# Pair building by single tiles, with a bucket's products kept in PSUM and its room read from a table

## The chip, the cores and the metric

The kernel runs on one core of a Trainium2 chip. The metric is the device time of one launch in microseconds (us). The engines are named as in the profile: PE (TensorE, with PEld for its weight loads), DVE (VectorE), ACT (ScalarE), POOL (GpSimd) and SP (the DMA queue). Each has a sequencer that takes its instructions in order; register instructions, loads of registers and waits are done there, and the profile marks them with a q (PEq, PEldq, DVEq).

## The reference, cut to what matters

Four graph layers work on 625 nodes of 512 features and 20000 edges. Every layer sums over edges into the node an edge ends in. The first two layers (a mean over neighbours, and two relational convolutions) need the edges only through sums over node pairs:

```python
# layer 0: mean over neighbours
neighbor_sum = segment_sum(x[src], dst)
h = concatenate([x, neighbor_sum / max(count, 1)]) @ W.T + b
# layer 1, twice: relational convolution, 8 relations, 4 bases
hb = einsum('nd,bdo->bno', h, basis)
m = sum_b comp[etype, b] * hb[b][src] * norm
out = segment_sum(m, dst) + bias + h @ loop_w
```

So the kernel builds nine matrices over (src, dst) once: for each of 2 x 4 coefficients the sum of `comp[etype, b] * edge_weight` over the edges of a node pair, and the count of edges. Layers 0 and 1 are then dense products with them. Layers 2 and 3 go over the edges by gathers and are not touched by the change.

## The kernel before

The program is a list of stages (`STAGES`, L2695): `constants`, `place_edges`, `order_pairs`, `build_pairs`, `layers_0_and_1`, `layers_2_and_3`. Between two stages all engines meet at a barrier (L2708). Inside a stage each engine has its own list of instructions, written out by hand, and semaphores order them.

The nodes an edge can end in are cut into 40 buckets of 16 (`CELL`): 5 blocks of 8. `place_edges` counts the edges of each bucket, gives each edge a slot of the sorted order, and a place (lane, tile) among tiles of 128 edges for the pair building. A bucket takes whole items of two tiles (`PAIR` = 256 edges), so `NI` = 118 items and `PT` = 236 tiles. It also writes `column_of_item`, which bucket an item belongs to, into one row of int32.

`order_pairs` brings keys, weights and coefficients of the edges into tile order with one-hot matmuls (20 batches, DVE writes the one-hots at L591 to L603, PE multiplies, ACT writes a third kind at L539) and computes from them, 236 columns wide, the nine values of each edge (`pair_high`, bf16, and `pair_rest`, fp16, what bf16 leaves). Beside it ACT and POOL clear `pairs` (L485, L532), and POOL sends the first `FIRST` = 54 columns of edge records to DRAM (`scatter_records`, L686).

`build_pairs` (L706) is the stage of the change. `pg.pairs` is 128 sources x 5 source blocks x 9 matrices x 640 ends, f32 in SBUF. For item g:

- DVE (L799) and, for the second tile in three items of four, ACT (L776, L780) write `src_hot`, the one-hot of each edge's source, 128 x 640.
- POOL (L765) writes `cell_high` and `cell_rest`: the one-hot of the end within its bucket times the nine (eight) values.
- PE (L741, L744) multiplies, for each of two tiles and five source blocks, `src_hot` by both: 20 matmuls of 144 or 128 columns, into one of two PSUM buffers `pairs_ps`.
- DVE loads the item's column from `column_of_item` into a register (L804) and adds the 720 columns of PSUM to `pairs` at that column (L809).

Semaphores: `used` (PE is done with an item), `cells_made`, `first_hot`, `second_hot`, and `added` (the PSUM buffer is free again). The loops are hardware loops (`Fori`), four items in a round.

Later, in layer 3, PE loads registers in the same form: `value_load` at L1919, twice in a row, and then computes a matmul operand's address from each (L1936).

Of the kernel before, what the change touches and what calls it, by code (L numbers as in the profile page):

```python
# [12 lines left out]
FP32 = mybir.dt.float32  # L13
BF16 = mybir.dt.bfloat16
# [28 lines left out]
PAIR = 2 * P  # L43
NI = (EDGES + NB * (PAIR - 1)) // PAIR + NB * (P // CELL - 1)
NI += (2 - NI) % 4
PT = 2 * NI
EARLY = EC // 2
LANDED = EC // 2
FIRST = 54
# [24 lines left out]
def constants(pg):  # L74
# [3 lines left out]
    pg.iota_src = pg.sb("iota_src", [P, PW], FP16)  # L78
    pg.iota_lane = pg.sb("iota_lane", [P, PT], BF16)
# [38 lines left out]
    pg.column_of_item = pg.sb("column_of_item", [1, NI], I32, pg.pair_once)  # L118
# [17 lines left out]
    with nc.semaphore("filled") as filled, nc.Block() as block:  # L136

        @block.gpsimd
        def _(pool):
            nc.gpsimd.iota(pg.iota_free[:, :], [[1, P]], base=0, channel_multiplier=0,  # L140
                           allow_small_or_imprecise_dtypes=True)
            nc.gpsimd.iota(pg.iota_lane[:, :], [[1, PT]], base=0, channel_multiplier=0,
                           allow_small_or_imprecise_dtypes=True)
            nc.gpsimd.iota(pg.iota_src[:, :], [[BN, NB], [1, P]], base=0, channel_multiplier=0,
# [21 lines left out]
def place_edges(pg):  # L166

    nc = pg.nc
    with ExitStack() as ctx:
# [32 lines left out]
        reached = pg.sb("reached", [P, BUCKETS], ctx=ctx)  # L202
        bucket_of = pg.sb("bucket_of_item", [P, 1], ctx=ctx)
        row_ps = ctx.enter_context(nc.psum_tensor("row_ps", [P, 512], FP32))
        table_ps = ctx.enter_context(nc.psum_tensor("table_ps", [P, 512], FP32))
# [28 lines left out]
        def _(pool):  # L234
            nc.gpsimd.iota(bucket_no[:, :], [[1, BUCKETS]], base=0, channel_multiplier=0,
                           allow_small_or_imprecise_dtypes=True)
            nc.gpsimd.iota(pg.iota_twice[:, :, :], [[1, PT], [0, 2]], base=0, channel_multiplier=0,
                           allow_small_or_imprecise_dtypes=True)
# [21 lines left out]
        def _(act):  # L260
# [23 lines left out]
            for ends, at in ((pg.edge_record[0:EP, 0:EARLY, SRC:SRC + 2], slice(0, EARLY)),  # L284
                             (pg.late_ends, slice(EARLY, EARLY + FIRST)), (pg.last_ends, slice(EARLY + FIRST, EC))):
                nc.scalar.copy(ends[:, :, 0], ints[:, 0, at])
                nc.scalar.activation(ends[:, :, 1], ints[:, 1, at], ACT.Identity, bias=pg.ones[0:EP, 0:1])

        @block.tensor
        def _(pe):  # L290
# [5 lines left out]
            nc.tensor.matmul(table_ps[0:1, 0:P], bucket_of[:, :], pg.ident[:, :], start=True,  # L296
                             stop=True).then_inc(sem["tables_turned"], 1)

        @block.vector
        def _(dve):  # L300
# [10 lines left out]
            for b in range(2, NB):  # L311
# [56 lines left out]
            link(nc.vector.tensor_scalar(bounds_i[:, 1, :], bounds[:, 1, :], float(PAIR - 1), None, ALU.add))  # L368
            link(nc.vector.tensor_scalar(bounds_i[:, :, :], bounds_i[:, :, :], 8, None, ALU.arith_shift_right))
            link(nc.vector.tensor_copy(bounds[:, :, :], bounds_i[:, :, :]))  # L370
            link(nc.vector.tensor_tensor(items[:, :], bounds[:, 1, :], bounds[:, 0, :], ALU.subtract))
            link(nc.vector.scalar_tensor_tensor(out=items[:, :], in0=total[:, :], scalar=0.0, in1=items[:, :],
                                                op0=ALU.is_gt, op1=ALU.mult))
            link(nc.vector.tensor_tensor_scan(out=item_last[:, :], data0=items[:, :], data1=zero[:, :],
                                              initial=0.0, op0=ALU.add, op1=ALU.add))
            nc.vector.tensor_scalar(reached[:, :], item_last[:, :], pg.lane_no[:, 0:1], None, ALU.is_le)
            link(nc.vector.tensor_tensor(offset[:, :], bounds[:, 0, :], item_last[:, :], ALU.subtract))
            nc.vector.tensor_reduce(bucket_of[:, :], reached[:, :], AX.X, ALU.add).then_inc(sem["tables_made"], 1)
            link(nc.vector.tensor_tensor(offset[:, :], offset[:, :], items[:, :], ALU.add))
            link(nc.vector.scalar_tensor_tensor(out=shift[0:EP, :], in0=offset[0:EP, :], scalar=float(P),  # L380
                                                in1=unit_size[0:EP, :], op0=ALU.add, op1=ALU.mult))
            link(nc.vector.tensor_tensor(shift[0:EP, :], shift[0:EP, :], start[0:EP, :], ALU.add))
            link(nc.vector.tensor_tensor(shift[0:EP, :], shift[0:EP, :], row_ps[0:EP, 0:BUCKETS], ALU.add))
            for b in range(BUCKETS):
# [19 lines left out]
            nc.vector.scalar_tensor_tensor(out=pg.pair_tile[:, :], in0=unit[:, :], scalar=-2.0,  # L404
                                           in1=slot_i[:, :], op0=ALU.mult, op1=ALU.add)

            dve.wait_ge(sem["tables_turned"], 1)
# [2324 lines left out]
```

## Time and profile before

| | us |
|---|---|
| median of 3 runs | 2236.05 |
| lowest, highest | 2234.85, 2241.26 |
| the profiled execution | 2239.19 |
| its span, first to last instruction | 2237.5 |
| `build_pairs` in it, barrier to barrier (188.0 to 383.3) | 195.3 |
| `order_pairs` in it, barrier to barrier (65.4 to 188.0) | 122.6 |

Busy time is given by engine; a PE matmul's listed duration runs from its start to its modelled end, and several are under way at once, so the spacing of starts tells what one costs. The times of the stages are read from the barrier's instructions. A stage ends when its last engine arrives.

### The profile page before, as it was taken

How to read it: one execution, taken by the hardware profiler on the slowest of the kernel's cores; microseconds unless marked ns; L12 is line 12 of the kernel's file. 1: busy time of each engine (PE TensorE's matmuls, PEld its weight loads, DVE VectorE, ACT ScalarE, POOL GpSimd, SP SyncE). 2: the span in 40 equal slices, each digit the busy share in tenths (PEclk: the TensorE clock that was granted, in tenths of full speed). 3: DMA queues.
4: the chain of work that ended last, by engine and by line, in shares of the span. 5: the costliest groups of instructions: out<-in, count | busy, mean ns of one | idle time of the engine just before them, and what ended most of it. 6: DMA issues, size and time to landing. Idle time of an engine off the chain costs nothing. (4 is left out here: it accounts for less than half of the span.)

```text
span 2237.5 us, 35489 instructions
## 1 busy us (share of the span) xinstructions
PE 1957.2 (87%) x11394; PEld 1133.0 (51%) x11507; DVE 1573.5 (70%) x2245; ACT 1274.9 (57%) x2059; POOL 1473.2 (66%) x1123
## 2 busy tenths in 40 slices
PE   0796887989898769999999978999999999999875
PEld 0775776456565524444444444555555555555432
DVE  8998998633333557777777743888888888888723
ACT  1667777021122246666666633777877777777622
POOL 1787777777600057777777713799889898998530
PEclk9999999989999879999999989999999999999988
DMA  2411001132234234333333204332222222222000
GB/s 117 161 22 46 0 0 43 35 106 60 64 106 113 61 108 140 109 95 93 90 94 90 80 11 128 97 95 76 72 83 72 78 74 71 83 73 77 5 0 23
DMA packets 78495, 165.22 MB, mean 74 GB/s; under 512 B 15999, under 2 KB 41016, under 8 KB 77220
## 3 DMA queue, kind: packets, MB, share of 16 engines
q0 software_dynamic: 34560, 94.69, 15.7%
q1 hardware_dynamic: 43800, 68.78, 9.4%
q8 instruction: 79, 1.29, 0.2%
q14 instruction: 56, 0.46, 0.1%
HBM read 139.86 MB, written 23.39 MB: 73 GB/s over the span
## 5 line engine op out<-in xcount | busy, mean ns | idle before, releaser
L939 PE MATMUL e_two_ps<-w,e_first 128*128 128x512 bf16 x1261 | 382.8, 380 | 4.7 <-issue 0.4
L686 POOL DMA_INDIRECT sorted_records<-edge_record,slot_row x160 | 248.4, 1552 | 69.1 <-issue 54.9
L2371 POOL DMA_INDIRECT e_got<-src_table,e_idx x168 | 225.8, 1344 | 67.2 <-issue 34.1
L939 PE MATMUL e_two_ps<-w,e_first_low 128*128 128x512 bf16 x672 | 255.2, 380 | 0.0
L1707 ACT ACTIVATE u_msg<-u_t,slot_record 128x128 f32<-128x128 f32 x672 | 214.4, 395 | 71.4 <-DVE u_t L1772 71.4
L1888 POOL TENSOR_TENSOR e_first_low<-e_first 128x1024 bf16<-128x1024 f32 x84 | 232.2, 2765 | 19.3 <-DVE e_first L2072 14.9
L1620 POOL TENSOR_TENSOR total<-total,u_part 125x1024 f32 x84 | 198.0, 2357 | 66.9 <-ACT u_part L1715 57.5
L1893 POOL TENSOR_TENSOR e_msg_low<-e_act 128x1024 bf16<-128x1024 f32 x84 | 189.3, 2253 | 39.1 <-DVE e_act L2084 37.7
L1610 POOL DMA_INDIRECT u_got<-up_table,u_idx x168 | 162.0, 964 | 60.0 <-POOL u_idx L1604 32.5
L939 PEld LDWEIGHTS e_two_ps<-w,e_first 128*128 128x128 bf16 x1344 | 128.3, 98 | 141.9 <-issue 2.2
L2079 DVE TENSOR_TENSOR e_lin<-e_two_ps,bias 128x512 f32<-128x512 f32 x168 | 115.3, 687 | 118.4 <-PE e_two_ps L939 118.4
L1671 PE MATMUL u_sum_ps<-u_msg,u_hot 128*125 128x512 f32 x336 | 179.9, 617 | 14.4 <-ACT u_msg L1707 14.4
L741 PE MATMUL pairs_ps<-cell_high,src_hot 128*128 128x144 bf16 x1180 | 152.8, 227 | 41.8 <-DVE src_hot L799 21.9
L1673 PE MATMUL u_sum_ps<-u_msg,u_hot 128*125 128x512 f32 x336 | 172.5, 595 | 0.0
L1997 ACT ACTIVATE e_act<-e_act,log_bias 128x1024 f32<-128x1024 f32 x84 | 96.5, 1148 | 104.7 <-DVE e_act L2061 104.7
L744 PE MATMUL pairs_ps<-cell_rest,src_hot 128*128 128x128 f16 x1180 | 152.2, 220 | 0.0
L741 PEld LDWEIGHTS pairs_ps<-cell_high,src_hot 128*128 128x128 bf16 x1180 | 115.4, 98 | 58.0 <-POOL cell_rest L765 55.7
L1366 PE MATMUL rc_out<-pairs 125*125 125x512 bf16 x600 | 135.6, 379 | 1.2 <-PE rc_mix L939 0.2
L1772 DVE TENSOR_TENSOR u_t<-u_tp_ps,u_got 128x256 f32<-128x256 f32 x168 | 70.6, 420 | 90.9 <-PE u_tp_ps L1660 88.9
L1444 DVE TENSOR_TENSOR pairs<-rc_mix,pairs 125x512 bf16<-125x512 f32 x40 | 27.7, 691 | 149.1 <-ACT pairs L1412 149.1
L1993 ACT ACTIVATE e_act<-e_lin 128x1024 f32<-128x1024 f32 x84 | 88.9, 1058 | 68.1 <-DVE e_lin L2079 68.1
L809 DVE TENSOR_TENSOR pairs<-pairs,pairs_ps 128x720 f32 x118 | 106.4, 902 | 21.5 <-PE pairs_ps L744 14.2
(373 smaller groups left out, 4725.6 us busy)
## 6 DMA issues: line engine op xcount, KB each, us to landing
conv_w<-in_L_gnn_basis_dram SPq DMA_DIRECT2D x8, 1024.0 KB
sorted_records<-pairs SPq DMA_DIRECT2D x5, 1344.0 KB, 10.4
later_w<-in_L_gnn_W_dram SPq DMA_DIRECT2D x6, 1024.0 KB
attr_parts<-h SPq DMA_DIRECT2D x21, 256.0 KB, 2.1
e_attrT<-attr_parts SPq DMA_DIRECT2D x42, 128.0 KB
e_dst_all<-dst_row SPq DMA_DIRECT2D x42, 125.0 KB
edge_record<-in_edge_floats_dram SPq DMA_DIRECT2D x1, 3125.0 KB
pairs<-in_edge_floats_dram SPq DMA_DIRECT2D x1, 3125.0 KB
```

What stands on the lines that cost most here:

```text
L686: pg.nc.gpsimd.indirect_dma_start(out=pg.sorted, out_offset=bass.IndirectOffsetOnAxis(ap=pg.slot_row[:, j:j + 1], axis=0), in_=pg.edge_rec ...
L741: nc.tensor.matmul(ps[h][:, sb, 0:(COEFS + 1) * CELL], hot, high[:, h, k, :, :].rearrange("p n d -> p (n d)"), start=(k == 0 and sb % 2 == ...
L744: last = nc.tensor.matmul(ps[h][:, sb, 0:COEFS * CELL], hot, rest[:, h, k, :, :].rearrange("p n d -> p (n d)"), start=False, stop=(k == 1 ...
L939: last = nc.tensor.matmul(out, lhsT, rhs, start=(n == 0), stop=(n == len(pairs) - 1))
L1610: nc.gpsimd.indirect_dma_start(out=got[:, b, :], out_offset=None, in_=tableU, in_offset=bass.IndirectOffsetOnAxis(ap=idx[:, r, k:k + 1], a ...
L1620: nc.gpsimd.tensor_tensor(into, into, part[:, n % 2, :], ALU.add).then_inc(added, 1)
L1671: nc.tensor.matmul(sum_ps[k // TH][0:BN, 0:D], hot[:, g % HOTS * TG + k, :], msg[:, k, 0:D], start=(k % TH == 0), stop=(k % TH == TH - 1))
L1673: nc.tensor.matmul(sum_ps[k // TH][0:BN, D:M], hot[:, g % HOTS * TG + k, :], msg[:, k, D:M], start=(k % TH == 0), stop=(k % TH == TH - 1)) ...
L1707: last = nc.scalar.activation(msg[:, k, at * MUL:(at + 1) * MUL], t12[:, k % 2, of], ACT.Copy, scale=pg.record[:, bass.ds(t, 1), Y + m])
L1888: nc.gpsimd.tensor_tensor(first_low[:, r % 2, 2 * u:2 * u + 2, :], full, upper(full), ALU.subtract).then_inc(low1, 1)
L1893: nc.gpsimd.tensor_tensor(msg_low[:, u, :, :], act2[:, u, :, :], upper(act2[:, u, :, :]), ALU.subtract).then_inc(low2, 1)
L2371: pg.nc.gpsimd.indirect_dma_start(out=self.got[:, r * TG + k, :], out_offset=None, in_=table, in_offset=bass.IndirectOffsetOnAxis(ap=self. ...
```

## The change

- Items of two tiles go. A bucket takes whole tiles of 128 edges and at least one: `PT` = 196 tiles.
- A bucket's products stay in PSUM over all its tiles. `pairs_ps` is one tensor of three rooms, each two banks (three source blocks in one, two in the other). Two rooms are used in turn by the buckets; room 0 takes what is not wanted.
- Which bucket a tile belongs to is known only from the data, so `place_edges` writes `tile_table`, four int32 for each tile: how many buckets must have been copied out, the tile's room, the room to open and the room to close (0 where the bucket goes on). PE loads the four into registers for each tile. A matmul of two columns (`mark`) opens or closes each bank, so a tile has 10 products and 4 marks.
- ACT copies a bucket out once, two copies for 40 buckets each, after loading from `tiles_through` the tile that ends it. DVE's additions and loads go, so `pairs` need not be cleared: POOL's and ACT's clearing in `order_pairs` goes.
- DVE writes `src_hot` for every tile; ACT writes none. Six buffers of it, three pairs of cell buffers.
- 42 columns of records are sent in `order_pairs` and 12 in `build_pairs`, one after every third pair of tiles.
- All loops of the stage are written out.

```diff
-PAIR = 2 * P
-NI = (EDGES + NB * (PAIR - 1)) // PAIR + NB * (P // CELL - 1)
-NI += (2 - NI) % 4
-PT = 2 * NI
+PT = (EDGES + NB * (P - 1)) // P + NB * (P // CELL - 1)
+PT += PT % 2
-FIRST = 54
+FIRST, IN_ORDER = 54, 42
...
-    pg.column_of_item = pg.sb("column_of_item", [1, NI], I32, pg.pair_once)
+    pg.tile_table = pg.sb("tile_table", [1, 4, PT], I32, pg.pair_once)
+    pg.tiles_through = pg.sb("tiles_through", [1, BUCKETS], I32, pg.pair_once)
...
+            nc.vector.tensor_scalar(pg.tiles_through[:, :], item_last[0:1, :], 1.0, None, ALU.add)
...
+            link(nc.vector.tensor_scalar(by_tile[:, 1, :], before_i[:, :], 1.0, None, ALU.add))
+            nc.vector.tensor_tensor(by_tile[:, 2:4, :], changed[:, :, :], by_tile[:, 1:2, :].broadcast_to([P, 2, 2]),
+                                    ALU.mult).then_inc(sem["tables_made"], 1)
...
             nc.gpsimd.memset(zero[:, :], 0.0).then_inc(zeroed, 1)
-            nc.gpsimd.memset(pairs[:, 0:CLEARED], 0.0)
             pool.wait_ge(pg.emptied, 16 * 5)
-            scatter_records(pg, range(0, FIRST))
+            scatter_records(pg, range(0, IN_ORDER))
...
-                if i >= WAITED:
-                    act.wait_ge(pg.emptied, 16 * 5)
-                    at = CLEARED + (i - WAITED) * size
-                    clear(pairs[:, at:at + size])
...
+            def mark(room, bank, begins):
+                at = slice(room, room + 1) if isinstance(room, int) else bass.ds(room, 1)
+                return nc.tensor.matmul(ps[:, at, bank, BANK * WIDE:BANK * WIDE + 2].rearrange("p r c -> p (r c)"),
+                                        pg.ident16[:, :], pg.ident16[:, 0:2], start=begins, stop=not begins)
+
+            def of_tile(k, t, top):
+                return nc.tensor.value_load(pg.tile_table[0:1, k, t:t + 1], min_val=1 if k == 0 else 0, max_val=top)
...
+            for t in range(PT):
+                before = of_tile(0, t, BUCKETS)
+                room = of_tile(1, t, 2)
+                opened = of_tile(2, t, 2) if t >= 1 else room_of(0)
+                closed = of_tile(3, t, 2) if t + 1 < PT else room_of(BUCKETS - 1)
+                pe.wait_ge(cells_made, t // 2 + 1)
+                pe.wait_ge(hots_made, t + 1)
+                pe.wait_ge(freed, before)
+                for bank in range(2):
+                    mark(opened, bank, True)
+                    for sb in range(bank * BANK, min(NB, (bank + 1) * BANK)):
+                        hot = src_hot[:, t % DEEP, sb * P:(sb + 1) * P]
+                        for cells in (high, rest):
+                            begin = sb % BANK * WIDE
+                            into = ps[:, bass.ds(room, 1), bank, begin:begin + cells.shape[3] * CELL]
+                            nc.tensor.matmul(into.rearrange("p r c -> p (r c)"), hot,
+                                             cells[:, t // 2 % TWO, t % 2, :, :].rearrange("p n d -> p (n d)"),
+                                             start=False, stop=False)
+                    last = mark(closed, bank, False)
                 last.then_inc(used, 1)
...
+            for b in range(BUCKETS):
+                if b + 1 < BUCKETS:
+                    through = nc.scalar.value_load(pg.tiles_through[0:1, b:b + 1], min_val=1, max_val=PT + 1)
+                    act.wait_ge(used, through)
...
+                    last = nc.scalar.copy(pg.pairs[:, sbs, :, b * CELL:(b + 1) * CELL],
+                                          full.rearrange("p (s n d) -> p s n d", n=COEFS + 1, d=CELL))
+                last.then_inc(freed, 1)
...
+            for t in range(PT):
+                if t >= DEEP:
+                    dve.wait_ge(used, t - DEEP + 2)
+                nc.vector.tensor_scalar(src_hot[:, t % DEEP, :], names, pg.pair_src[:, t:t + 1], None,
+                                        ALU.is_equal).then_inc(hots_made, 1)
```

On PE, where an item begins inside `build_pairs`, this stands before (L738 and L749 are register instructions for the semaphore's value, ISA is such an instruction):

```order
L741 MATMUL pairs_ps<-cell_high,src_hot 128x144 [waits pairs_first_hot,pairs_added,pairs_cells_made]
L744 MATMUL pairs_ps<-cell_rest,src_hot 128x128
L741 MATMUL pairs_ps<-cell_high,src_hot 128x144
L744 MATMUL pairs_ps<-cell_rest,src_hot 128x128
L741 MATMUL pairs_ps<-cell_high,src_hot 128x144
L744 MATMUL pairs_ps<-cell_rest,src_hot 128x128
```

And this stands on PE after the change where a tile begins (the second tile; `tile_table` is the table, L733 the marks, L757 the products):

```order
L737 TENSOR_LOAD tile_table
L737 ISA x2
L737 TENSOR_LOAD tile_table
L737 ISA x2
L737 TENSOR_LOAD tile_table
L737 ISA x2
L737 TENSOR_LOAD tile_table
L737 ISA x2
L733 ISA [waits pairs_freed,pairs_hots_made,pairs_cells_made]
L733 MATMUL pairs_ps<-ident 128x2
L757 ISA
L757 MATMUL pairs_ps<-cell_high,src_hot 128x144
```

Four loads, each with two register instructions behind it, now stand in front of every tile's first matmul; the rest of the tile is nine single ISA instructions (the two last rows' kind) with 14 matmuls among them.

On DVE the same stage before, one item of the loop:

```order
L799 ISA [waits pairs_used]
L799 TENSOR_SCALAR src_hot<-pair_names_ps,pair_src 128x640
L804 ISA
L804 TENSOR_LOAD column_of_item
L804 ISA x2
L806 REGISTER_ALU
L809 ISA [waits pairs_added,pairs_used]
L809 TENSOR_TENSOR pairs<-pairs,pairs_ps 128x45x16
```

and on ACT after, the first two buckets:

```order
L785 ACTIVATE h<-x,x_nmr,x_rs 125x512 x5
L789 TENSOR_LOAD tiles_through
L789 ISA x2
L796 COPY pairs<-pairs_ps 128x27x16 [waits pairs_used]
L796 COPY pairs<-pairs_ps 128x18x16
L789 TENSOR_LOAD tiles_through
```

The load with its two register instructions has left DVE, where it stood once for two tiles; ACT has one for each bucket, and PE four for each tile.

## Rows read from the trace of the kernel before

**Rows 1.** Windows (order_pairs, build_pairs): stretch, busy us of engines, clock, DMA:

```profile
core 0: us, PE busy (x) PEld busy (x) DVE busy (x) ACT busy (x) POOL busy (x), PEclk, DMA share, GB/s
65.00:187.00 122.00, 105.38 (x843) 85.29 (x843) 115.62 (x202) 82.12 (x215) 99.50 (x56) 0.97 0.21 65
188.00:383.30 195.30, 157.67 (x2360) 142.00 (x2360) 171.84 (x265) 151.11 (x185) 146.47 (x236) 0.99 0.03 11
```

**Rows 2.** Waits in 188 to 383: who for whom, us, times, longest:

```profile
PEld pairs_ps L741 <- POOL cell_rest L765: 55.7, 88, 9.5
POOL cell_high L765 <- PE pairs_ps L744: 42.7, 87, 1.6
PE pairs_ps L741 <- DVE src_hot L799: 21.9, 57, 0.6
```

**Rows 3.** Tile pairs_ps: operation, count, ns min/median/max, first and last start us:

```profile
L741 PE MATMUL pairs_ps<-cell_high,src_hot x1180: 222/226/328, 189.8 to 380.2; 128*128 128x144 bf16 x197
L809 DVE TENSOR_TENSOR pairs<-pairs,pairs_ps x118: 894/904/906, 192.4 to 380.6; 128x720 f32 x118
```

**Rows 4.** Timeline of PE, first and last of an item's 20 matmuls:

```profile
282.53 0.22 PE L741 MATMUL pairs_ps<-cell_high,src_hot 128*128 128x144 bf16 x1 [0.38 <-POOL cell_rest L765]
...
283.65 0.22 PE L744 MATMUL pairs_ps<-cell_rest,src_hot 128*128 128x128 f16 x1
```

**Rows 5.** Lines L765 (POOL) and L799 (DVE), columns as in Rows 3:

```profile
L765 POOL TENSOR_TENSOR cell_high<-pair_cell,pair_high x118: 666/669/673, 188.5 to 377.8; 128x288 bf16 x118
L765 POOL TENSOR_TENSOR cell_rest<-pair_cell,pair_rest x118: 611/614/617, 189.1 to 378.4; 128x256 f16 x118
L799 DVE TENSOR_SCALAR src_hot<-pair_names_ps,pair_src x147: 541/545/550, 188.2 to 378.5; 128x640 bf16<-128x640 bf16 x147
```

**Rows 6.** Line L1919, PE's register loads in layer 3, all of them:

```profile
L1919 PEldq TENSOR_LOAD <-block_of_half x168: 295/298/486, 1372.1 to 2089.3; - x168
L1919 PEldq FUSED_REGOPS  x168: 151/151/165, 1372.6 to 2089.6; - x168
L1919 PEldq SEQ_ASSERT  x168: 18/18/32, 1372.9 to 2089.8; - x168
```

**Rows 7.** Line L1919 in 1599 to 1601, one pair of loads in a row:

```profile
L1919 PEldq TENSOR_LOAD <-block_of_half x2: 298/298/298, 1599.4 to 1600.0; - x2
L1919 PEldq SEQ_ASSERT  x2: 18/18/18, 1600.0 to 1600.6; - x2
```

**Rows 8.** Line L1936 in 1600.5 to 1601.5, the address instructions behind that pair:

```profile
L1936 PEldq FUSED_REGOPS  x4: 51/58/65, 1600.7 to 1601.1; - x4
```

**Rows 9.** Tile count_ps, 50 matmuls of one column in a row:

```profile
L939 PE MATMUL count_ps<-ones,pairs x50: 165/165/187, 388.2 to 389.6; 125*128 125x1 bf16 x50
```

**Rows 10.** Line L804, DVE's register loads in build_pairs:

```profile
L804 DVEq TENSOR_LOAD <-column_of_item x118: 298/305/566, 188.7 to 378.9; - x118
```

**Rows 11.** Lines by form, an ACT copy out of PSUM, busy us and mean ns:

```profile
L565 ACT CAST pair_high<-pair_coef_ps 128x472 bf16<-128x472 f32 x2 | 1.9, 1058 | 0.0
```

**Rows 12.** Timeline, the first of the 54 records' scatters, the last, DVE's last:

```profile
77.38 1.37 POOL L686 DMA_INDIRECT sorted_records<-edge_record,slot_row  x1 [0.73 <-DMA sorted_records<-pairs]
...
183.13 1.18 POOL L686 DMA_INDIRECT sorted_records<-edge_record,slot_row  x1 [0.30 <-issue]
...
184.15 0.66 DVE L679 TENSOR_TENSOR pair_rest<-hT,pair_high 128x472 f16<-128x472 f32 x1 [0.21 <-ACT pair_high L567]
```

**Rows 13.** Lines L593 and L664 (DVE in order_pairs), columns as in Rows 3:

```profile
L593 DVE TENSOR_TENSOR pairs<-hT,pair_tile x20: 1133/1134/1137, 66.2 to 147.2; 125x1888 bf16<-125x1888 bf16 x20
L664 DVE SCALAR_TENSOR_TENSOR hT<-h,pair_comp,hT x28: 452/462/515, 169.2 to 181.0; 128x236 f32<-128x236 f32 x28
```

**Rows 14.** Timeline, an iota that goes, and a small DVE operation of place_edges:

```profile
1.41 0.68 POOL L144 IOTA iota_src<- 128x640 f16 x1
...
60.88 0.24 DVE L399 TENSOR_SCALAR key_part_i<-h 125x160 int32<-125x160 int32 x1
```

## What the change should do to the time

> **What bounds the kernel now.** I read the windows view first, by stage. `build_pairs` lasts 195.3 us, and in it no engine is full: DVE 172, PE 158, ACT 151, POOL 146 us [rows 1]. The waits view says why: the engines wait on each other in a ring, PE's weight loads for POOL's `cell_rest` 55.7 us, POOL for PE 42.7 us, PE for DVE's `src_hot` 21.9 us [rows 2]. Each has two buffers. The first and last of DVE's 118 additions give 188.2 / 117 = 1.61 us for an item [rows 3]. PE's own need is smaller: a listed matmul lasts 226 ns, but 20 of them start within 282.53 to 283.65, so one costs 1.12 / 19 = 0.059 us [rows 4] and an item 1.18 us. The end of the chain of waits lies in layer 3, behind barriers; each stage is a piece of the sum of its own, so I work by stages and read in each which engine comes last.
>
> **What the matmuls, one-hots and copies cost after the change.** There are 196 tiles instead of 236. PE's array has ten products at 0.059 us and four marks. A mark is nearest to the 50 one-column matmuls that start within 388.2 to 389.6, 0.029 us each, weights loaded anew each time [rows 9]. That is 0.59 + 0.12 = 0.71 us a tile, 139 us in all. POOL has 98 pairs of tiles at 0.669 + 0.614 us = 126 us [rows 5], and twelve scatters of about 1.2 us [rows 12], together 140 us. DVE has 196 operations at 0.545 us = 107 us at most [rows 5], and its additions (118 x 0.904 = 107 us) are gone [rows 3]. ACT has 80 copies. No row shows one of 432 or 288 f32 columns into strided places; by the copy of 472 columns at 1.06 us [rows 11] a bucket costs at most 2.1 us, 85 us in all, and it lies beside 4.9 tiles of PE's work thanks to the two rooms. Only the last bucket's copies are on the path. So far the stage would end at POOL's and PE's 140 us.
>
> **What PE's sequencer costs after the change.** This is the term I put the forecast on. In front of every tile stand four `value_load`s on PE. `build_pairs` of before has none on PE, but layer 3 has 168 of just this form there, always two in a row. One load is a TENSOR_LOAD of 298 ns, a register instruction of 151 ns and an assertion of 18 ns, 0.467 us [rows 6]. With the gaps between them it is more: the two loads start at 1599.4 and 1600.0, the second assertion at 1600.6, and the first address instruction behind at 1600.7 [rows 7, 8]. Two loads thus took 1.3 us, 0.65 us each. They run one behind the other and overlap with nothing on the sequencer. In layer 3 they are hidden because the array has many 512-column matmuls queued; here the whole array work of a tile is 0.71 us. Four loads are 2.60 us a tile.
>
> Then come nine address instructions, each in front of one or two matmuls that are handed over. Four of these start within 1600.7 to 1601.1, three spacings in 0.4 us, one weight load and matmul in each [rows 8]: 0.14 us. Nine are 1.26 us. Five more matmuls at 0.03 us [rows 9] are 0.15 us, and the separate wait instruction about 0.05 us. The sequencer needs 2.60 + 1.26 + 0.15 + 0.05 = 4.06 us for a tile, against 0.71 us of the array. A queue cannot help, since every tile has the same surplus. 196 x 4.06 = 796 us. To that I add 3.5 us for the first loads' fill, the last bucket's copies and the barrier: 799 us for the stage, 604 us more than 195.3. DVE, POOL and ACT wait for PE and cost nothing; should the clock granted to a PE that idles this much be 1.2 GHz instead of 2.4, the array's 0.71 us doubles to 1.4 and still hides.
>
> The price of a load has ends. From below, if the gaps vanished: 4 x 0.467 us, and nine address instructions at their own 0.058 us [rows 6, 8], with 14 matmuls at 0.03: 1.87 + 0.52 + 0.42 = 2.81 us a tile. From above, the slowest load in any row, DVE's 566 ns [rows 10], every time: 4 x (0.65 - 0.298 + 0.566) + 1.46 = 5.13 us. Nothing below zero is open: the instructions are added and DVE's removed loads lay beside other work. I take 0.65 because rows 7 and 8 are the same engine and the same three instructions. Read with the rounding of those rows (0.1 us on 1.3 and on 0.4), a load is 0.60 to 0.70 and an address instruction 0.10 to 0.17, which makes 3.5 to 4.5 us a tile.
>
> The Trainium skill, "DMA: Bandwidth & Descriptors", section on latency and other measured facts, gives `tensor_load` a floor of about 600 ns, to be amortized by unrolling. The trace does not agree with that as the duration of the instruction (298 ns), though it nearly does for the whole sequence of 0.65 us. By the page's figure as a duration, an estimate from it: 4 x (0.65 - 0.298 + 0.600) + 1.46 = 5.27 us a tile, 237 us above my sum.
>
> **The stages ahead.** In `order_pairs` two engines end close together: POOL's 54 scatters run from 77.38 to 183.13, 2.0 us each, and DVE's last operation ends at 184.8 [rows 12], while the barrier opens at 188.0 [rows 1]. A barrier alone takes at most 1.8 us (383.3 less the last addition's end at 381.5 [rows 1, 3]), so it was POOL's last records that it waited for. With 42 scatters POOL is done by about 160, so DVE sets the end. DVE loses by width: 1568 elements instead of 1888 in 20 operations of 1.134 us, at most 0.19 each or 3.8 us [rows 13]; and of the 28 operations of 0.462 us and some thirty others, all 236 wide and now 196, I count 0.05 each, 3.5 us with `pair_cell`. So DVE ends at about 177.5, the barrier opens by 179.3 at the latest, and that is 9 us earlier. The clearing goes from POOL and ACT, but POOL waited for the emptied DRAM anyway (the first scatter's releaser is a DMA [rows 12]), and ACT waited for DVE; nothing for that. `constants` loses two iotas, 1 us by the row of 0.68 [rows 14]; `place_edges` gains some eight small DVE operations at up to 0.24 [rows 14], hidden to about half by SP's issues: 1 us. PE's transposes of the table lie beside DVE. Sum ahead: -9 to -10 us. Layers 0 to 3 have the same instructions, behind a barrier as before; nothing for them.
>
> **Sum.** 2237.5 + 604 - 10 = 2831.5 us of span. The profiled run took 2239.2, which is 3.1 above the median of 2236.05, so against the median: 2236 + 594 = **2830 us**.
>
> **The rivals.** *The loads hide (ends on the other side).* Place: PE's sequencer between two tiles. If it could hand over a tile's loads while the array works, such that what is not hidden is under (195.3 - 3.5) / 196 = 0.98 us a tile, the stage would not get longer. Fully hidden, the stage ends by POOL's and PE's 140 us and 7 for fill and gaps, 147: 2236 - 48 - 10 = 2178 us. For it speaks that in rows 6 layer 3 loses nothing to its loads, and that the code keeps a tile's work together. Against it: there they have 20 matmuls of over 0.2 us to hide behind, here 14 of 0.05. Chance 0.06.
>
> *Cheap sequencer (still slower).* The gaps vanish where the array is idle, 2.81 us a tile: 551 + 3.5 us, 2236 + 359 - 10 = 2585 us. Against it: in rows 7 and 8 the sequencer was not held up by the array either, for the loads need no place in its queue. Chance 0.04.
>
> *Dear loads.* The slow loads of rows 10 are the rule: 5.13 us a tile, 1009 us, 2236 + 814 - 10 = 3040 us. The median of 298 over 168 loads speaks against it. Chance 0.03. By the floor in the Trainium skill, "DMA: Bandwidth & Descriptors", section on latency and other measured facts, an estimate of this kind comes to 3067 us.
>
> *The change does not do what it says.* The instruction order shows the four loads, the 14 matmuls and the 80 copies, so this I leave at nothing.
>
> **How the numbers follow.** The forecast, sequencer bound at about 4 us a tile, has 0.87. Its own range by 3.5 to 4.5 us a tile is 2830 - 110 to 2830 + 90, rounded out to 2715 to 2930; I give that 0.93 within the case, so the range holds 0.81 and need not reach to the rivals. The measurement can tell about 0.3% of the time (7 us) from no change. Slower by more: 0.87 + 0.04 + 0.03 = 0.94, less 0.01 for a mixed case that ends on par. Same: 0.01. Faster: 0.06.
>
> **What would show it.** Right: `build_pairs` near 800 us; L737 with 782 TENSOR_LOADs on PE's sequencer near 0.3 us, starting 0.65 us apart; PE busy a fifth of the stage or less between bursts, with POOL and DVE waiting for PE at L776 and L808, and ACT's buckets some 20 us apart. `order_pairs` shorter by about 9 us with DVE last. Wrong: matmuls of successive tiles without gaps, waits of PE for POOL as the longest, or loads that start closer than 0.5 us. If the array's work showed as the longer one, with the clock at its lower level and matmuls over 0.2 us apart, the place would be right and the mechanism wrong. If a later stage changed by over 5 us, the sum by stages would be wrong.

## The result and the profile after

The changed kernel takes 2798.4 us (median of 4 runs, 2793.45 to 2799.39) against 2237.1 us before (4 runs, 2234.85 to 2241.26). The ratio is 1.250, with a 95% interval of 1.248 to 1.253. The prediction was 2830 us with a range of 2715 to 2930.

The windows view of after, by stage (constants and `place_edges` together, `order_pairs`, `build_pairs`, the layers); its columns are those of [rows 1]:

```profile
core 0: us, PE busy (x) PEld busy (x) DVE busy (x) ACT busy (x) POOL busy (x), PEclk, DMA share, GB/s
0.00:62.70 62.70, 4.64 (x20) 2.77 (x20) 53.74 (x111) 13.53 (x19) 8.13 (x28) 0.88 0.34 143
62.70:174.40 111.70, 92.04 (x843) 77.23 (x843) 106.84 (x201) 65.72 (x198) 66.40 (x43) 0.93 0.21 70
174.40:942.30 767.90, 294.90 (x2749) 257.59 (x2750) 107.48 (x197) 36.75 (x87) 136.22 (x209) 0.50 0.01 4
942.30:2797.70 1855.40, 1702.36 (x8298) 905.03 (x8298) 1233.10 (x1673) 1029.07 (x1641) 1217.56 (x802) 0.96 0.28 79
```

and the same view of before for the layers, which [rows 1] leaves out:

```profile
383.30:2237.50 1854.20, 1692.54 (x8185) 904.74 (x8298) 1232.84 (x1673) 1028.86 (x1641) 1218.61 (x802) 0.96 0.28 79
```

The layers are the same within 1.2 us. The whole difference lies in one stage: `build_pairs` lasts 767.9 us where it lasted 195.3 [rows 1]. In it POOL is busy for 136 us, DVE for 107, ACT for 37, all less than before, and PE's 295 us of busy time cover 38% of it. No engine in the view is full. An engine's busy time leaves out what its sequencer does, and PE's sequencer is what is full here. The lines of PE's sequencer, by line (L737 the loads, L749 the wait, L733 the addresses of the marks, L757 those of the products), with count, ns min/median/max, first and last start in us:

```profile
L737 PEldq TENSOR_LOAD <-tile_table x782: 293/300/491, 174.6 to 937.6; - x196
L737 PEldq FUSED_REGOPS  x782: 146/151/165, 175.1 to 937.9; - x196
L737 PEldq SEQ_ASSERT  x782: 18/18/28, 175.3 to 938.2; - x196
L749 PEldq EVENT_SEMAPHORE  x196: 51/51/51, 176.7 to 938.3; - x196
L733 PEldq FUSED_REGOPS  x780: 46/53/65, 177.3 to 938.9; - x195
L757 PEldq FUSED_REGOPS  x980: 46/46/51, 176.8 to 939.1; - x196
```

The wait stands once in each tile: 938.3 less 176.7 over 195 is 3.906 us for a tile, where the forecast had 4.06. The same lines in one tile near the middle, in three windows: its loads, its wait and its nine addresses, and the loads of the next tile:

```profile
L737 PEldq TENSOR_LOAD <-tile_table x4: 296/297/301, 498.5 to 500.5; - x4
...
L749 PEldq EVENT_SEMAPHORE  x1: 51/51/51, 501.1 to 501.1; - x1
...
L757 PEldq FUSED_REGOPS  x5: 46/46/51, 501.4 to 502.1; - x5
...
L733 PEldq FUSED_REGOPS  x4: 46/53/65, 501.2 to 502.3; - x4
...
L737 PEldq TENSOR_LOAD <-tile_table x3: 303/303/305, 502.4 to 503.7; - x3
```

From the first load (498.5) to the wait (501.1) it is 2.6 us for four loads, 0.65 us each. The wait takes 0.1 us, and from the first address (501.2) to the next tile's first load (502.4) it is 1.2 us for nine addresses, 0.13 us each. All 14 matmuls of the tile are handed over in that time. The waits view of after, from 180 us on, says who stands still for it:

```profile
ACT pairs L796 <- PE pairs_ps L733: 729.5, 40, 22.7
DVE src_hot L808 <- PE pairs_ps L733: 634.8, 189, 3.5
POOL cell_high L776 <- PE pairs_ps L733: 605.5, 95, 6.7
PEld pairs_ps L733 <- issue: 499.3, 195, 2.7
PE pairs_ps L733 <- issue: 433.5, 180, 2.6
```

Three engines wait for PE, and PE waits for "issue", which means for nothing that the profile shows. The ring of [rows 2], in which each waited for the other, is gone. (The view puts 34.9 us in 15 tiles down to POOL: it names the one that came last of those that a tile asks for, and the sum of 2.6, 0.1 and 1.2 us leaves no room for a wait.) ACT has 40 waits of at most 22.7 us, one for each bucket. The timeline shows the burst of the tile above:

```profile
501.34 0.18 PE L733 MATMUL pairs_ps<-ident 128*128 128x2 bf16 x1 [2.46 <-issue]
501.47 0.30 PE L757 MATMUL pairs_ps<-cell_high,src_hot 128*128 128x144 bf16 x1
501.56 0.31 PE L757 MATMUL pairs_ps<-cell_rest,src_hot 128*128 128x128 f16 x1
...
502.63 0.21 PE L733 MATMUL pairs_ps<-ident 128*128 128x2 bf16 x1
```

2.46 us of nothing, then 14 matmuls within 1.29 us. Their starts are 0.10 us apart in the mean (those of two products in a row 0.08 to 0.12), where they were 0.059 us apart before [rows 4]. The granted clock in this stage is 0.50 (the windows view above), the lower of the two levels, 1.2 GHz. PE idled 2.5 us of every 3.9.

In `order_pairs`, 111.7 us in the windows view, the records end early and DVE ends last (timelines of POOL and DVE; [rows 12] before):

```profile
155.20 1.19 POOL L684 DMA_INDIRECT sorted_records<-edge_record,slot_row  x1 [0.30 <-issue]
...
172.50 0.57 DVE L677 TENSOR_TENSOR pair_rest<-hT,pair_high 128x392 f16<-128x392 f32 x1 [0.16 <-ACT pair_high L566]
```

Where a stage is timed from barrier to barrier by the barrier's own instruction on POOL, as in what follows, the numbers are: `order_pairs` 122.6 before and 110.6 after, `build_pairs` 195.3 and 767.8.

### The profile page after: what moved, and what is told of

It is laid out like the page before. It is cut to its first block and busy times, and to the rows that moved or that the text cites. A ratio compares the mean times of both kernels' runs of the same rounds, so it can differ in the third digit from the quotient of the medians.

```text
span 2797.7 us, 38255 instructions
## 1 busy us (share of the span) xinstructions
PE 2093.9 (75%) x11909; PEld 1242.6 (44%) x11909; DVE 1501.2 (54%) x2181; ACT 1145.1 (41%) x1945; POOL 1428.3 (51%) x1081
## 5 line engine op out<-in xcount | busy, mean ns | idle before, releaser
L733 PE MATMUL pairs_ps<-ident 128*128 128x2 bf16 x788 | 124.2, 193 | 475.3 <-issue 433.5
L808 DVE TENSOR_SCALAR src_hot<-pair_names_ps,pair_src 128x640 bf16<-128x640 bf16 x196 | 107.5, 550 | 637.3 <-PE pairs_ps L733 635.8
L928 PE MATMUL e_two_ps<-w,e_first 128*128 128x512 bf16 x1344 | 403.7, 382 | 0.0
L776 POOL TENSOR_TENSOR cell_high<-pair_cell,pair_high 128x288 bf16<-128x288 bf16 x98 | 65.5, 668 | 623.7 <-PE pairs_ps L733 605.5
L796 ACT COPY pairs<-pairs_ps 128x432 f32<-128x432 f32 x80 | 32.8, 462 | 729.5 <-PE pairs_ps L733 729.5
L733 PEld LDWEIGHTS pairs_ps<-ident 128*128 128x128 bf16 x788 | 100.7, 139 | 506.9 <-issue 506.9
L757 PE MATMUL pairs_ps<-cell_rest,src_hot 128*128 128x128 f16 x980 | 250.1, 314 | 0.0
L757 PE MATMUL pairs_ps<-cell_high,src_hot 128*128 128x144 bf16 x980 | 246.9, 312 | 0.1
L2360 POOL DMA_INDIRECT e_got<-src_table,e_idx x168 | 211.9, 1261 | 67.2 <-issue 33.9
L1882 POOL TENSOR_TENSOR e_msg_low<-e_act 128x1024 bf16<-128x1024 f32 x84 | 198.1, 2358 | 47.5 <-DVE e_act L2073 46.5
```

Of the source, the lines that this page charges most:

```text
L733: return nc.tensor.matmul(ps[:, at, bank, BANK * WIDE:BANK * WIDE + 2].rearrange("p r c -> p (r c)"), pg.ident16[:, :], pg.ident16[:, 0:2] ...
L757: nc.tensor.matmul(into.rearrange("p r c -> p (r c)"), hot, cells[:, t // 2 % TWO, t % 2, :, :].rearrange("p n d -> p (n d)"), start=False ...
L928: last = nc.tensor.matmul(out, lhsT, rhs, start=(n == 0), stop=(n == len(pairs) - 1))
L1882: nc.gpsimd.tensor_tensor(msg_low[:, u, :, :], act2[:, u, :, :], upper(act2[:, u, :, :]), ALU.subtract).then_inc(low2, 1)
L2360: pg.nc.gpsimd.indirect_dma_start(out=self.got[:, r * TG + k, :], out_offset=None, in_=table, in_offset=bass.IndirectOffsetOnAxis(ap=self. ...
```

## The experiments

**Theory:** the time of the stage is the time of PE's sequencer for a tile, the sum of its loads, its wait and its address instructions; nothing of it lies beside the array, and no other engine counts. **Rivals:** the lower clock or the structure with marks and long accumulation costs the time; the loads only wait for data; another engine's work is slow. The first five experiments take parts of that sum away one at a time, or put them into the kernel before. These five and the one after them were executed once each, so what they show rests on differences of many microseconds and on the stage times in their own traces.

### Two loads in place of four

```diff
-                opened = of_tile(2, t, 2) if t >= 1 else room_of(0)
-                closed = of_tile(3, t, 2) if t + 1 < PT else room_of(BUCKETS - 1)
+                opened = closed = room
```

> The changed kernel (2798 us) with two of PE's four register loads in front of each tile, and the room to open and to close taken from the tile's own room; it leaves out what a bucket's earlier tiles added, the rest of the work is the same. Seven address instructions in a tile instead of nine. Theory (PE's sequencer takes the loads one after the other, 0.65 us each, and 0.13 us for an address instruction, and the array's work hides behind): 2 x 0.65 + 2 x 0.13 = 1.57 us less in each of 196 tiles, 308 us less, 2490 us. Rival (the marks and the array at its lower clock set the pace): 14 matmuls as before, so 2798 us. Rival (what costs is a fixed latency for a group of loads, not each load): under 100 us less.

Measured: 2489.4 us, `build_pairs` 462.5 us. The loads (392 in place of 782) and the addresses of the marks, of which a tile now needs two in place of four:

```profile
L737 PEldq TENSOR_LOAD <-tile_table x392: 295/302/493, 175.2 to 632.8; - x196
...
L733 PEldq FUSED_REGOPS  x392: 46/56/65, 176.9 to 634.2; - x196
```

Two loads at 0.65 us and two addresses at 0.13 us are 1.56 us less, and 3.91 less 1.56 is 2.35 us a tile. The wait's instruction goes from 176.8 to 633.4, so the tile took 2.34 us. The array has the same 14 matmuls, and the clock is still 0.50:

```profile
180.00:630.00 450.00, 288.53 (x2695) 252.49 (x2693) 104.08 (x189) 32.30 (x80) 131.51 (x202) 0.50 0.02 7
```

So neither is the bound. The waits view of this kernel names DVE for PE's idle time (149.6 us in 179 waits). This is a way of counting: the wait asks for three things and the view names the one that came last of them. DVE itself waited 338.7 us for PE, and the loads, the wait and the addresses fill the 2.34 us by themselves.

### Three of the four loads without the check of their bounds

```diff
-                return nc.tensor.value_load(pg.tile_table[0:1, k, t:t + 1], min_val=1 if k == 0 else 0, max_val=top)
+                if k == 0:
+                    return nc.tensor.value_load(pg.tile_table[0:1, k, t:t + 1], min_val=1, max_val=top)
+                return nc.values_load(pg.tile_table[0:1, k, t:t + 1], engines=[mybir.EngineType.PE],
+                                      min_val=0, max_val=top,
+                                      skip_runtime_bounds_check_because="place_edges clamps every entry of the table")
```

> The changed kernel with all four loads, but three of them without the bound check (the register instruction of 151 ns and the assertion of 18 ns behind the load). Theory of single instructions in order: each unchecked load takes 0.36 us from its start to the next instead of 0.65, 3 x 0.29 = 0.87 us less in a tile, 170 us less, 2628 us. Rival (the load's answer is what is waited for, and loads in a row overlap when nothing reads their register): three loads in a row cost little more than one, up to 0.3 us less each, down to 2500 us. Rival (array or marks set the pace): 2798 us.

Measured: 2638.3 us, `build_pairs` 600.0 us. The stage is 167.8 us shorter, near the expected 170; the total is 10 us above the expectation mostly because the layers of this run were 7 us longer. The three loads of one tile, lines of PE's sequencer in 500 to 503.5:

```profile
L739 PEldq TENSOR_LOAD <-tile_table x3: 296/302/302, 501.5 to 502.2; - x3
```

Without the register instruction and the assertion behind it a load takes 0.36 us to the next one: 0.30 of its own and 0.06 of gap. So 0.29 of the 0.65 us were the check of the bounds, and the loads run one behind the other even where nothing stands between them: they start 0.36 us apart and last 0.30.

### One load that fills four registers

```diff
-    pg.tile_table = pg.sb("tile_table", [1, 4, PT], I32, pg.pair_once)
+    pg.tile_table = pg.sb("tile_table", [1, PT, 4], I32, pg.pair_once)
...
+                _, (before, room, opened, closed) = nc.values_load_multi_w_load_instructions(
+                    pg.tile_table[0:1, t, :], engines=[mybir.EngineType.PE], min_val=0, max_val=BUCKETS,
+                    skip_runtime_bounds_check_because="place_edges clamps every entry of the table")
+                before = nc.s_assert_within(before, 1, BUCKETS)
...
```

> The changed kernel with the table turned, so that one load fills all four registers of a tile, and only the value that PE waits against is checked (0 loads fewer in what they deliver, same results). Three unchecked loads cost 160 us less than checked ones. Theory (it is the number of load instructions that costs, 0.36 us each with its gap): one load and its check 0.65 us, nine address instructions 1.2 us, a wait 0.1 us, 1.96 us a tile against 3.91, 382 us less than 2798, so 2416 us. Rival (the price is for each register filled, so four in one cost four times the 0.3 us): 0.9 us more a tile, 2590 us. Still above the kernel before either way, since nine address instructions alone are 1.2 us a tile.

Measured: 2402.1 us, `build_pairs` 375.0 us. Of all tiles:

```profile
L743 PEldq TENSOR_LOAD <-tile_table x196: 327/331/525, 173.9 to 544.3; - x196
```

One load of four registers lasts 331 ns, 30 ns more than a load of one. 370.4 us over 195 is 1.90 us a tile: 0.39 us from the load to the next instruction, 0.17 for the assertion that is left, 0.11 for the wait and 1.20 for the nine addresses make 1.87. This halves the stage (375.0 of 767.8), takes back 396 of the 561 us that the change lost in all, and is still 163 us slower than before: nine addresses alone are 1.20 us a tile, 235 us in all, more than the whole stage of before.

### The rooms fixed when the kernel is built

```diff
+        def bucket_of(t):
+
+            return t * BUCKETS // PT
...
-                before = of_tile(0, t, BUCKETS)
-                room = of_tile(1, t, 2)
-                opened = of_tile(2, t, 2) if t >= 1 else room_of(0)
-                closed = of_tile(3, t, 2) if t + 1 < PT else room_of(BUCKETS - 1)
+                before = bucket_of(t) + 1
+                room = room_of(bucket_of(t))
+                opened = room if t == 0 or bucket_of(t - 1) != bucket_of(t) else 0
+                closed = room if t + 1 == PT or bucket_of(t + 1) != bucket_of(t) else 0
...
```

(the address of each product's room and what ACT waits for become constants in the same way)

> The changed kernel with rooms and waits written as constants, tile t in bucket t * 40 / 196 rounded down: no register loads and no address instructions on PE or ACT, all matmuls, marks, copies and one-hots as in the changed kernel, loops written out as in it. The sums land in the wrong bucket here and there, the amount of work is the same. Theory: the stage falls from 768 us to about 150, set by POOL's 140 us of cells and scatters and PE's array (0.71 us a tile), so 2180 us. Rival (the marks, the copies out of PSUM or the written-out loops are slow by themselves): the stage stays above 195 us and the time above 2225 us.

Measured: 2184.3 us, against 2240.7 for the kernel before on the same chip, and `build_pairs` 150.9 us. The stage in the windows view, and two waits in 180 to 325:

```profile
174.30:325.20 150.90, 139.78 (x2748) 138.41 (x2748) 107.32 (x196) 36.77 (x87) 135.28 (x208) 0.98 0.06 20
```

```profile
ACT pairs L799 <- PE pairs_ps L737: 112.7, 40, 3.6
DVE src_hot L811 <- PE pairs_ps L737: 12.3, 13, 1.1
```

PE does the same 2748 matmuls in this stage, and is busy for 139.8 us of 150.9, at a clock of 0.98. What is gone is register work, on PE and on ACT (one load for each bucket); which bucket a tile goes to is different, the amount of work is not. So it is the register work that took 617 us. The low clock came and went with it, and in the three experiments above the time fell by what was taken from the sequencer while the clock stayed at 0.50: it was not the cause. The rest of the change (marks, accumulation over a bucket, one copy on ACT, narrower tables, records moved) would have made the kernel faster by 56 us, 44 of them in this stage. It would need rooms that don't depend on the data, and here they do.

### The same four loads in the kernel before

```diff
+                for k in range(4):
+                    nc.tensor.value_load(pg.column_of_item[0:1, k:k + 1], min_val=0, max_val=(BUCKETS - 1) * CELL)
```

> The kernel before with four register loads on PE in front of every item of two tiles, whose values nobody uses; same results. Theory (sequencer time adds up and only the part beside which the array is busy is hidden): 2.6 us of loads and about 0.7 us of the item's own register and wait instructions against an item of 1.61 us, so 118 x 1.7 = 200 us more, about 2435 us (2400 to 2480 by what handing over 20 matmuls costs). Rival (loads hide in PE's queue behind 20 matmuls): 2237 us.

Measured: 2413.5 us, `build_pairs` 370.3 us where it was 195.3. The four loads of one item, lines of PE's sequencer in 400 to 402.8:

```profile
L733 PEldq TENSOR_LOAD <-column_of_item x4: 301/302/310, 400.2 to 402.2; - x4
L733 PEldq FUSED_REGOPS  x4: 146/146/146, 400.6 to 402.5; - x4
L733 PEldq SEQ_ASSERT  x4: 18/18/18, 400.8 to 402.7; - x4
```

The spacing is again 0.65 us. The item goes from 1.61 us to 3.1: 2.6 for the loads and 0.5 for the rest of what the sequencer does in an item. The 1.18 us of the array disappear beside it. Nothing of the changed kernel but its loads is in this one, and that does three tenths of its damage (175 us of 572), with 118 items in place of 196 tiles.

### All 54 columns of records in `order_pairs` again

```diff
-FIRST, IN_ORDER = 54, 42
+FIRST, IN_ORDER = 54, 54
```

> The changed kernel with order_pairs working on all 54 record columns again, as in the kernel before. Theory: POOL's records then end last again, and the stage goes from 110.6 us back to 116 or more, the time from 2798 to about 2803. Rival: the chain of DVE sets the end of the stage in the changed kernel whatever POOL does, and the stage stays within 1 us of 110.6 and the time at 2798.

Measured: 2801.1 us, `order_pairs` 117.2 us where it was 110.6, `build_pairs` 767.7. POOL's last record and DVE's last operation of the stage:

```profile
175.83 1.19 POOL L684 DMA_INDIRECT sorted_records<-edge_record,slot_row  x1 [0.30 <-issue]
...
172.41 0.57 DVE L677 TENSOR_TENSOR pair_rest<-hT,pair_high 128x392 f16<-128x392 f32 x1
```

DVE ends where it ended, POOL ends 4.0 us after it, and the stage is 6.6 us longer. So of the 12.0 us that the change gained in `order_pairs`, moving twelve records out made 6.6. The 5.4 that remain are POOL's in this run, since it ends the stage:

```profile
L684 POOL DMA_INDIRECT sorted_records<-edge_record,slot_row x54: 1182/1502/3569, 75.3 to 175.8; - x54
```

Its 54 scatters take 100.5 us from first to last start, and before they took 105.7 [rows 12]. Narrower tables and less clearing are both in this run, and which of them lets the scatters follow each other faster is not shown. In `build_pairs` the twelve records cost nothing: the stage was 767.8 with them and 767.7 without. The total moved by 2.7 us only (2798.4 to 2801.1), since the layers of this run were 4.7 us shorter, which is within what they differ from run to run.

### The kernel before, its ring made deeper

The last three ask what the ring of [rows 2] was worth without a table. Here the stage of before has three buffers for one-hots and cells instead of two, `src_hot` is written two items ahead, and the loops are written out; PSUM has its two buffers as before. ACT's five activations of `h` stand at the start of the stage and not at its end, and two small buffers lie in other memory.

```diff
-            src_hot = pg.sb("src_hot", [P, 2, 2, PW], BF16, ctx)
+            src_hot = pg.sb("src_hot", [P, RING_IN, 2, PW], BF16, ctx)
...
-                    pool.wait_ge(used, g + 1)
+                if g >= RING_IN:
+                    pool.wait_ge(used, g - RING_IN + 1)
...
+            for g in range(RING_IN - 1):
+                operand(g)
+            for g in range(NI):
+                if g + RING_IN - 1 < NI:
+                    operand(g + RING_IN - 1)
```

> The kernel before with three buffers instead of two for the one-hots of the sources and for the cells, the loops of the stage written out, nothing else. Theory (the ring of waits costs what the stage has above its fullest engine, and that is DVE with 147 x 0.545 + 118 x 0.90 = 186 us): the stage goes from 195 to 189 us, 2231 us, 6 us less. Rival (every item still waits for the addition that frees its PSUM buffer, so depth elsewhere gives nothing): 2237 us, no change.

Measured: 2218.3 us (2215.55 to 2219.87), 0.991 of the kernel before, interval 0.989 to 0.992. `build_pairs` takes 171.7 us, 23.6 less. The waits in it, and DVE in a stretch of its timeline:

```profile
PEld pairs_ps L750 <- POOL hT L769: 24.5, 30, 9.1
PE pairs_ps L750 <- POOL hT L769: 19.0, 29, 8.3
POOL cell_high L769 <- PE pairs_ps L753: 17.3, 30, 3.0
...
DVE pairs L817 <- PE pairs_ps L753: 5.9, 3, 5.2
```

```profile
270.36 0.96 DVE L817 TENSOR_TENSOR pairs<-pairs,pairs_ps 128x720 f32 x1
271.17 0.61 DVE L802 TENSOR_SCALAR src_hot<-pair_names_ps,pair_src 128x640 bf16<-128x640 bf16 x1
271.63 0.96 DVE L817 TENSOR_TENSOR pairs<-pairs,pairs_ps 128x720 f32 x1
272.44 0.61 DVE L802 TENSOR_SCALAR src_hot<-pair_names_ps,pair_src 128x640 bf16<-128x640 bf16 x1
```

The waits are down from 55.7 and 42.7 us [rows 2] to 24.5 and 17.3, and DVE runs without a gap. It is the bound now, but a lower one than I had put into the expectation: listed at 0.96 and 0.61 us, the two operations start 0.81 and 0.46 us apart. 118 x 0.81 + 147 x 0.46 is 163 us, not the 186 that their durations in [rows 3, 5] add up to.

### The same ring with work moved from DVE to ACT

ACT writes the second one-hot in seven items of eight in place of three of four, and twelve columns of records go to `build_pairs`, as in the change.

```diff
-FIRST, IN_ORDER = 54, 54
+FIRST, IN_ORDER = 54, 42
...
-        RING_IN, SHARE = 3, 4
+        RING_IN, SHARE = 3, 8
```

> As e5_deeper, and ACT writes the second one-hot in seven items of eight instead of three of four, and 12 of the 54 columns of records are sent inside the stage as in the changed kernel. Theory: DVE 132 x 0.545 + 118 x 0.90 = 178 us, ACT 104 x 1.66 + 6 = 178 us, POOL 151 + 18 = 169 us, so the stage goes to about 183 us; order_pairs ends with DVE instead of POOL's records, 2 us less: 2237 - 12 - 2 = 2223 us. Rival (ACT, slower at a one-hot, now holds each item up): the stage stays at 195 us or grows, 2235 us or more.

Measured: 2230.4 us (2228.55 to 2232.33), 0.996 of before, interval 0.995 to 0.997, and 12 us slower than the deeper ring alone. `order_pairs` gained 1.8 us and `build_pairs` takes 189.1. The stage's busy times and its waits:

```profile
186.00:375.10 189.10, 157.40 (x2360) 142.58 (x2360) 161.11 (x250) 175.94 (x215) 159.64 (x248) 0.97 0.05 16
```

```profile
DVE pairs L817 <- PE pairs_ps L753: 26.5, 39, 5.2
...
PEld pairs_ps L750 <- ACT src_hot L793: 22.4, 38, 2.9
```

ACT is busy for 175.9 us and PE waits for it; DVE, relieved of 15 operations, waits for PE. ACT itself waits for PE only 3.2 us in the whole stage: it is the bound. I had thought DVE the bound with 186 us and room to give. It had 163, and ACT writes a one-hot in two operations of 0.83 us that start 0.86 apart, 179 us for 104 of them. Whether the twelve scatters on POOL cost anything here, no run shows by itself.

### The kernel before, written out with its two buffers

```diff
-        RING_IN, SHARE = 3, 4
+        RING_IN, SHARE = 2, 4
```

(against the deeper ring, so that against before the hardware loops are gone, and ACT's activations and two buffers have moved)

> The kernel before with build_pairs written out, so that no hardware loop runs over the buckets, and with the same two buffers as before; order_pairs and all later stages are those of before. Theory: it is the ring of two buffers that holds the tiles in lock step, so the stage stays at 185 us or more and the time at 2230 or more. Rival: it is the hardware loops (their branches and the addresses computed in them) that cost the stage its time, so that writing it out with two buffers gives what the deeper ring gave: about 172 us for the stage and 2218 us in all.

Measured: 2241.4 us (10 runs), ratio 1.0007 to before, interval 0.9996 to 1.0018; `build_pairs` 198.1 us. Its waits:

```profile
PEld pairs_ps L750 <- POOL hT L769: 52.9, 59, 9.0
POOL cell_high L769 <- PE pairs_ps L753: 45.7, 59, 4.2
```

The same waits as in [rows 2], about the same lengths. The hardware loops cost nothing that shows, and the third buffer (with the one-hots written further ahead) gives the whole gain of the deeper ring.

## Why the prediction was right, and where it was off

**The bound.** It named PE's sequencer as what would set the time of `build_pairs`, by four loads of 0.65 us one behind another. The trace shows 0.65 us; fixing the rooms took away 617 us, putting only the loads into the kernel before added 175. The span is 34 us under the forecast one (2797.7 against 2831.5): 31 by this stage, nearly 4 by the stages ahead, and about 1 us the other way by the layers.

**The terms of a tile.** Four loads: 2.60 predicted, 2.60 measured. Nine address instructions: 1.26 predicted (0.14 each, from three spacings in 0.4 us whose ends are rounded to a tenth), 1.20 measured. Five more matmuls at 0.03: 0.15 predicted, nothing measured. This term was the one with a wrong idea in it: a second matmul behind an address is handed over in the time that the address takes anyway. The wait: 0.05 predicted by its own duration, 0.11 measured with the gap behind it. Sum 4.06 against 3.91. That the net is just the 0.15 of the matmuls is chance, since the other two misses cancel. 0.15 x 196 is 29 of the 31 us by which the stage came out shorter (767.8 against 799).

**The cover.** DVE, POOL, ACT and the array at half clock were said to hide, and did. The burst at the lower clock lasts 1.3 us, as the text allowed (1.4). "PE busy a fifth of the stage" was wrong: it is 38%, 1.3 to 1.5 us of every 3.9, since at this clock the 14 matmuls start 0.10 us apart and not 0.06.

**The higher figure for a load.** By the floor that the Trainium skill states for `tensor_load` ("DMA: Bandwidth & Descriptors", section on latency and other measured facts) the text had estimated 5.27 us a tile. The loads lasted 300 ns (median of 782) and the tile 3.91 us, so the trace goes against that figure as a duration.

**The stages ahead.** The sum was -10 us for the three stages, and it was -13.6. `order_pairs` gave 12.0 instead of 9, and DVE ended it, as said; the run with all 54 columns shows that 6.6 of them need the records moved and 5.4 come without. DVE's last operation ended at 173.1 where I had 177.5. Of these 4.4 us, 1.6 are the stage's earlier start. The other 2.8 are a wait that I had not counted: at a batch's end DVE waits for PE to free the one-hots' buffer. The groups of DVE that stand behind this wait, before and after:

```profile
L591 DVE TENSOR_TENSOR pair_lane_hot<-hT,pair_lane 125x1024 bf16<-125x1024 bf16 x20 | 13.8, 692 | 5.2 <-PEq L491 3.0 <-PE pair_slots_ps L513 1.3
...
L590 DVE TENSOR_TENSOR pair_lane_hot<-hT,pair_lane 125x1024 bf16<-125x1024 bf16 x20 | 13.7, 683 | 2.4 <-PEq L500 1.6 <-PE pair_slots_ps L522 0.8
```

From the start of the operation before it to its own start it was 0.795 us in the mean of 19 batches and is 0.648, which makes 2.8 us. PE's matmuls there are 196 columns wide and no more 236, and PE's busy time in the stage fell from 105.4 us [rows 1] to 92.0. That it therefore frees the buffer sooner fits, but no run takes it apart from the rest. The widths on DVE itself are as counted: the operation of [rows 13] fell by 0.168 us (at most 0.19 said), `pair_cell` from 4.084 to 3.410. `place_edges` was put at +1 us and gave -0.7, so its eight small operations do not show in its time.

**The rivals.** Hidden loads (2178) and a cheap sequencer (2585) fell by the same number, the 0.65 us: the gaps between a load and its successor are there, the array idle or not. What hidden loads would have given is near the 2184 us of the kernel with fixed rooms, in which there are none to hide. Dear loads (3040) fell with the median of 300 ns; a few of 491 ns exist.

## What to carry to other kernels

A register read from memory on an engine's sequencer is work of that engine, though its busy time does not show it: count loads, checks and address instructions for each round and compare their sum with the array's work in that round, before choosing a table over a fixed plan. Where a table is needed, load a round's registers with one instruction, leave the check of bounds out where the values are clamped already, and keep operands' addresses constant. Where engines wait for each other in a ring, try a third buffer before a new structure: here it gave 0.9%.

## What the runs showed of the hardware that I had not expected

- A load of four registers lasts 331 ns and a load of one 300 ns; the check of bounds costs 0.29 us a load, about as much as the load.
- An address instruction (46 to 65 ns) comes at 0.12 to 0.14 us from the next instruction, and one or two matmuls behind it add nothing to that.
- PE at 38% of busy time, in bursts of 1.3 us in every 3.9, was granted a clock of 0.50 over the whole stage. The loads in the kernel before, with PE busy 229 of 365 us, left it at 0.70. With one load for a tile PE is listed as busy for 289 of 365 us and the clock is 0.50 as well, where the kernel before has 158 of 195 us [rows 1] at 0.99: the listed share alone does not tell the clock, since at the lower level the same matmuls are listed for longer.
- Successive operations on DVE overlap: in the deeper ring a listed 0.96 us starts 0.81 before its successor, and a listed 0.61 only 0.46. A bound from listed durations was 186 us where the starts gave 163.
